# VectorE's copy of the decay columns as a tensor_reduce, and the clip of the decays read from PSUM

## What is computed

```python
beta = jnp.clip(jax.nn.sigmoid(x @ Wg + bg), 0.8, 0.9995)   # one decay per token and head
def step(carry, inp):
    S, z = carry
    S = S * b_t[..., None, None] + pk_t[..., :, None] * v_t[..., None, :]
    z = z * b_t[..., None] + pk_t
    numer = jnp.einsum('bhd,bhde->bhe', pq_t, S)
    denom = jnp.sum(pq_t * z, axis=-1, keepdims=True) + EPS
    return ((S, z), numer / denom)
```

## Time and profile before

| | before |
|---|---|
| median of 3 runs | 944.36 us (943.74 to 944.86) |
| span of the profiled execution | 923.8 us |
| TensorE busy, share of the span | 824.6 us, 89% |
| TensorE weight loads | 763.2 us, 83% |
| VectorE | 670.7 us, 73% |
| GpSimd | 595.3 us, 64% |
| ScalarE | 522.2 us, 57% |

### The profile page before, as it was taken

How to read it: one execution, slowest core, us unless ns; L and a number is a source line. 1 busy time by engine, 2 the same in 40 slices (tenths; PEclk the granted TensorE clock), 3 DMA queues, 4 the chain that set the end, 5 groups by cost and what they waited for, 6 DMA issues and landing times. The chain is left out here.

```text
span 923.8 us, 26887 instructions
## 1 busy us (share of the span) xinstructions
PE 824.6 (89%) x8382; PEld 763.2 (83%) x8382; DVE 670.7 (73%) x2155; ACT 522.2 (57%) x1357; POOL 595.3 (64%) x698
## 2 busy tenths in 40 slices
PE   4778975999999977999998999988899999999795
PEld 3768875999999966787787778877899999999795
DVE  3788772777878556889898988986566777777253
ACT  4644531566666436777667768755433666666231
POOL 4788775476676525776889888876431766776440
PEclk9899977999999998999999999999999999999998
DMA  6747224344444455246344342153414455553799
GB/s 189 209 131 226 80 91 133 100 128 128 129 139 129 97 80 59 32 44 112 93 82 114 67 111 81 50 144 109 175 38 145 127 176 156 154 174 110 124 197 250
DMA packets 79542, 113.50 MB, mean 123 GB/s; under 512 B 9488, under 2 KB 67696, under 8 KB 78256
## 3 DMA queue, kind: packets, MB, share of 16 engines
q0 software_dynamic: 34208, 56.65, 26.7%
q1 hardware_dynamic: 45200, 55.13, 21.7%
HBM read 59.49 MB, written 52.26 MB: 121 GB/s over the span
## 5 line engine op out<-in xcount | busy, mean ns | idle before, releaser
L969 POOL DMA_INDIRECT expert_out<-MEM,YIDX x142 | 147.0, 1035 | 99.6 <-ACT MEM L1109 97.6
L1527 PE MATMUL PSA<-EGUh,MEMR 128*128 x568 | 172.3, 345 | 4.6 <-DVE MEMR L1308 2.9
L935 POOL DMA_INDIRECT expert_rows<-MEM,POSU x128 | 127.5, 996 | 53.1 <-issue 32.1
L1470 PE MATMUL PSA<-MEMR,SGUh 128*128 128x256 f32 x720 | 152.7, 296 | 1.9 <-DVE SGUl L1176 1.8
L1470 PEld LDWEIGHTS PSA<-MEMR,SGUh 128*128 128x128 f32 x720 | 119.7, 191 | 4.1 <-DVE SGUl L1176 2.3
L1077 ACT ACTIVATE MEM<-PSA 128x256 f32<-128x256 f32 (+1 forms) x96 | 36.6, 381 | 138.8 <-PE PSA L1470 77.2
L1527 PEld LDWEIGHTS PSA<-EGUh,MEMR 128*128 128x128 f32 x568 | 102.8, 188 | 7.4 <-issue 6.7
L1485 PE MATMUL PSA<-SDh,MEMR 128*128 128x256 f32 (+1 forms) x384 | 88.0, 294 | 21.5 <-DVE MEMR L1250 10.8
L1470 PE MATMUL PSA<-MEMR,SGUl 128*128 128x256 f32 x360 | 105.1, 292 | 0.0
L1241 DVE TENSOR_TENSOR MEM<-PSA,MEM 128x256 f32<-128x256 f32 (+1 forms) x96 | 40.3, 420 | 79.1 <-ACT MEM L1077 79.0
L1527 PE MATMUL PSA<-EGUl,MEMR 128*128 x284 | 91.4, 322 | 0.0
(11 more groups left out here) (177 smaller groups left out, 2446.5 us busy)
## 6 DMA issues: line engine op xcount, KB each, us to landing
MEM<-expert_rows SPq DMA_DIRECT2D x142, 130.0 KB
X<-expert_out POOLq DMA_DIRECT2D x32, 512.0 KB, 6.3
rows_turned<-EGUl SPq DMA_DIRECT2D x7, 1024.0 KB, 4.3
MEMR<-rows_turned SPq DMA_DIRECT2D x14, 512.0 KB, 6.1
X<-in_L_attn_x SPq DMA_DIRECT2D x8, 512.0 KB, 6.0
X<-in_L_attn_bo POOLq DMA_DIRECT2D x8, 512.0 KB, 9.6
out<-X SPq DMA_DIRECT2D x8, 512.0 KB, 4.6
expert_rows<-FILL SPq DMA_DIRECT2D x30, 130.0 KB
```

The costliest lines, as they stand in the source:

```text
L935: pool.indirect_dma_start(out=rows_d[n.f], out_offset=bass.IndirectOffsetOnAxis(ap=POSU[:, k, i:i + 1], axis=0), in_=XN[n.xn][:, c, :], in ...
L969: pool.indirect_dma_start(out=y_d[f], out_offset=bass.IndirectOffsetOnAxis(ap=YIDX[:, j % 8:j % 8 + 1], axis=0), in_=YS[j % 3], in_offset= ...
L1470: last = mm(t[0:h, w * HALF:(w + 1) * HALF], SGU[b][:, w, k, j * P:j * P + h], XT[slot][a][:, k, hf * HALF:(hf + 1) * HALF], start=i == 0, ...
L1527: last = mm(t[:, 0:2 * HE], XGR[j % 2][a][:, k, :], EGU[b][:, bass.ds(e, 1), k, :], start=i == 0, stop=i == 3 * KD - 1)
```

## The change

ScalarE's second instruction of `beta_tanh` writes its result into the PSUM bank of `beta`, where the first one read, and no longer into BT. The clip reads PSUM, writes BT, and frees the bank; before, the tanh freed it. ScalarE waits for its own tanh through a new semaphore. And L1381 becomes a sum over an added axis of length one, which leaves the same numbers.

```diff
-                a(BT, t[:, 0:P], ACT.Tanh, bias=HBG[:, 0:1], scale=0.5).then_inc(free(("beta", g)), 1)
-                taken(act, ("beta", g))
-                a(BT, BT, ACT.Copy, scale=0.5, bias=0.5).then_inc(s_bt, 1)
+                a(BT, t[:, 0:P], ACT.Tanh, bias=HBG[:, 0:1], scale=0.5).then_inc(s_bth, 1)
+                act.wait_ge(s_bth, g + 1)
+                a(t[:, 0:P], BT, ACT.Copy, scale=0.5, bias=0.5).then_inc(s_bt, 1)
...
                 dve.wait_ge(s_bt, g + 1)
-                v.tensor_scalar(BT, BT, BETA_MIN, BETA_MAX, ALU.max, ALU.min)
+                v.tensor_scalar(BT, PS[at["beta", g].bank][:, 0:P], BETA_MIN, BETA_MAX, ALU.max, ALU.min).then_inc(free(("beta", g)), 1)
...
-                v.tensor_copy(va[:, :, DH], idec).then_inc(s_va, 1)
+                v.tensor_reduce(va[:, :, DH], idec.unsqueeze(2), AX.X, ALU.add).then_inc(s_va, 1)
```

More of the change, by code:

```diff
@@ L654, in build @@
         s_boa = [sem(f"bo_added{g}") for g in range(NG)]
-        s_wt, s_bt = sem("weights_ready"), sem("gate_ready")
+        s_wt, s_bt, s_bth = sem("weights_ready"), sem("gate_ready"), sem("gate_tanh_done")
         s_start, s_half = sem("attend_cleared"), sem("gate_halved")
```

## The result

| kernel | median | runs | ratio to before (95% interval) |
|---|---|---|---|
| before | 944.61 us | 4 (943.74 to 946.40) | |
| changed | 930.95 us | 4 (927.02 to 933.25) | 0.9864 (0.9830 to 0.9898) |

The change saves 13.7 us by the medians and 12.9 by the ratio. The forecast was 10, with 927 to 944.5 as its range.

A forecast was written before the change was run, and what follows sets the result against it. In the attention TensorE (busy 270.75 of 295 us) was nearest its limit, VectorE close behind, leaving 24.25 us idle to gain. 4.7 + 5.3 + 1.5 = 11.5, less 1.5, gave 10 us: 934.4 us, range 927 to 944.5.

The forecast's parts named there:

- R3: Rival at L1381: the reduce waits for GpSimd as the copy does, leaving 1.6 us gained, 942.8 us; chance 0.06.
- Part (a): Attention: TensorE's direct waits for VectorE at L1445, L1565, L1558 and L1617 all go, 4.7 us.
- Part (b): Attention: TensorE's waits at L1629 and L1452 shrink as GpSimd's L994 no longer waits for L1396, 5.3 us.
- Part (c): TensorE's 2.96 us wait at L1651 for VectorE's stalled L1235 was a toss, taken as 1.5 us gained.
- R1: Rival: the stall moves to VectorE's two-input router steps in the attention, slower at 953.7 us; chance 0.10.
- R2: Rival: TensorE's waits belong to the order, not VectorE, and return later; no change, 943.5 to 944.4 us; chance 0.09.
- my 1.5: Attention: 1.5 us taken off the gain because TensorE, once ahead, meets ScalarE and GpSimd earlier.
- R4: Rival: all of (a), (b) 7.3, (c) 3.0 and 3.6 us of clock are gained, 18.6 us, 925.8 us; chance 0.13.
- R4's clock: From 600 to 640 us the granted clock, 0.91 before, stays up, giving 3.6 us within R4.
- The 20.6 us around the span: Time outside the profiled span of 923.8 us, added to the predicted span of 913.8 to give 934.4 us.

The follow-up runs named there:

- job 1: Runs on one chip: kernel before twice, reduction alone, clip alone, changed kernel with two plain reductions ahead; before took 939.76 us.
- reordered kernel: Kernel before with L1380 and the copy L1381 placed behind L1396 in VectorE's queue; 912.84 us, ratio 0.9873.
- two plain reductions ahead: Changed kernel with two added reductions of 512 constants ahead of L1381 in each tile; 935.55 us, ratio 0.9950 to before.
- job 2: Runs on one chip: kernel before, changed kernel with two inputs, two copies or one plain reduction, and the reordered kernel; before took 924.50 us.
- the kernel with two inputs: Changed kernel with L1381 as a tensor_tensor, inverse decays times a column of ones; 925.74 us, ratio 1.0013 to before.
- job 3: Runs on one chip: kernel before, changed kernel, and it with v_copy behind L1396, one plain reduction, or two and v_copy behind; before took 940.15 us.
- one plain reduction: Changed kernel with one added reduction of 512 constants ahead of L1381 per tile; 907.22 us (ratio 0.9815) in job 2, 929.50 us (0.9881) in job 3.
- two copies: Changed kernel with L1381 as two tensor_copies, of 15 columns and of 1; 925.12 us, ratio 1.0015 to before.

## Why the prediction was right, point by point

- **That L1381's duration was a wait for GpSimd, and that a reduction has none:** right. 175 ns forecast, 172 in the median, 175 at most. R3 falls.
- **The clip:** 276 ns forecast, 292 measured. I had 6.5 us less of VectorE's time. What I missed is that the wait can move to the instruction behind: the scan L1343 reads two SBUF inputs and went from 461 to 568 ns in the median and 971 at most. That and the clip's 16 ns are 1.3 of the 3.3 us by which VectorE's saving in the first pair fell short. For the result the clip is worth nothing that could be measured; R3 had priced it at 1.6 us.
- **ScalarE into PSUM and the later freeing of the bank, at nothing:** right. L1119 took 282 ns in place of 311, and no wait of TensorE is put down to the clip, which now frees the bank.
- **Part (a), 4.7 us for TensorE's direct waits for VectorE:** the waits went (5.2 us in job 1, over the stage), but my reason for them is in doubt. I wrote that VectorE was late by its own copies and would catch up. In the reordered kernel the copies still wait, and L1445's wait is gone too. It is also gone with two plain reductions ahead, where GpSimd still waits 10.3 us for L1396. What made VectorE late at L1445 is therefore not shown, neither its copies nor GpSimd.
- **Part (b), 5.3 us through GpSimd's L994:** this is the main mechanism, and I had sized it wrongly. Moving the copy behind L1396 gave 11.7 us alone, and nothing more on top of the reduction. I had looked for it in two of TensorE's waits only, L1629 and L1452, and in job 1 these gave just 3.4 us over the stage: the rest of what GpSimd's wait cost came out elsewhere.
- **Part (c), L1235's 3.61 us as a toss:** it is no toss. The stall comes back in both kernels of job 2 in which the copy's place still waits, 3597 and 3602 ns at 610 us (the line below is the kernel with two inputs), each time with L1651's long wait behind it. In job 1 the kernel before had 1936 ns there. In the kernels with a reduction it is absent from the attention, but for 1929 ns with two plain reductions ahead. So it depends on where VectorE stands when it comes there, and it comes back in the same kind of execution. R1 did not happen: L1221 and L1191 were as long before.

```profile
L1235 DVE TENSOR_TENSOR MEM<-CS,MEM x6: 218/221/3597, 425.4 to 610.4; 128x32 f32<-128x32 f32 x6
```

- **R2, that the waits are the order's:** not as I meant it, since the waits did not come back under other names. But most of what was gained hung on the order of a few instructions in VectorE's queue, and that could be changed.
- **The sum:** 10 us forecast, 13.7 measured, 12.9 by the ratio, and 0.9880, 11.3 us, in job 3 (10.5 by the medians). Part by part in job 1, over the stage: (a) 5.2 us for 4.7, (b) 3.4 for 5.3, (c) 1.2 for 1.5, and 2.0 us of new waits for ScalarE (L1052 and L1147) for my 1.5. That is 7.8 us. Small waits at L1605, L1660 and elsewhere bring it to the 8.8 us by which TensorE's idle time fell. The other 2.2 us are less busy time, which I had put at nothing.
- **Luck in the number:** I read the waits from an execution of job 2's kind and they were priced against times of the other kind. In job 2's kind more was to be had: the kernel with one plain reduction, the nearest to the changed one there, gained 17.3 us, close to R4's 18.6. That 10 us fits the result so well is in part this exchange, as far as can be told without the changed kernel itself in job 2.
- **R4's clock:** from 600 to 640 us the granted clock is 1.00 in the changed kernel, but also in the kernel before once more. So in this kind of execution there was none of R4's 3.6 us to gain. In job 2 the kernels with two inputs and with two copies have 0.96 there and the one with a plain reduction 1.00.
- **The 20.6 us around the span:** wrong. They are 1.7 to 1.8 us. The forecast of the time took them off and put them back, so they did no harm to it.

What stays open: in job 2, one plain reduction with the changed kernel's form gave 17.3 us and the reordering 11.7 us. The changed kernel itself was not run in that job, so whether VectorE's time is worth the other 5.6 us there is not known. Nor was it followed up why TensorE stands 3.0 to 4.3 us at L1637 near the end of the stage in one kind of job, for every form of the kernel, and not in the other. The profile puts it down to ScalarE's L1147 in some of them and to nothing that it shows in the rest.

## What to carry to other kernels

A duration that varies by a factor of ten for one shape is a wait that no list of waits shows; find the engine whose instruction ends with it. Then ask what stands behind the waiting instruction in its queue and who waits for that. Here most of the loss was not the 35 us that VectorE stood still, but the 0.78 us in each of 19 tiles for which GpSimd, the very engine it had waited for, then waited for VectorE. Such a pair can be opened by another instruction or by another place in the queue: each gained over 1%, and the two together no more than the first. And before subtracting two spans, or two lists of waits, make sure that both profiles are of the same kind of execution.

## What the runs showed of the hardware

A reduction over an axis of one is a copy that doesn't wait for GpSimd: 166 to 177 ns in eight profiles of six kernels, 32 times each. A tensor_tensor with two SBUF inputs (172 to 2515 ns) and a copy of 15 columns (169 to 2525 ns) wait as the copy of 16 did. ScalarE writes 128 x 128 numbers into PSUM in 282 ns and into SBUF in 311 ns. A copy that waits ends 37 to 54 ns after GpSimd's L981, in 25 of 25 cases of the first profile. The same kernel took 939.8, 924.5 and 940.2 us in three jobs, so that only ratios within a job can be compared. The record has the first two jobs on a chip of one number and the third on another, so that it is the chip which differs, as two of my expectations say, is not shown.
